# Two kinds of copies on ScalarE placed elsewhere in the attention loop of a gated cross-attention block with a mixture of experts

## What is computed

```python
x = x + tanh(g_xattn[0]) * xattn(layernorm(x), ctx, Wq, Wk, Wv, Wo, q_norm_w, k_norm_w, pos_ctx, pos_x)
x = x + tanh(g_ffn[0])  * ffn(layernorm(x), w_router, w_gate, w_up, w_down, ws_gate, ws_up, ws_down)

# xattn: 16 query heads of 128 in 4 groups, one key head and one value head for each group
q = rope(rms_norm((x_n @ Wq.T) per head)); k = rope(rms_norm((kv_in @ Wk.T) per head)); v = kv_in @ Wv.T
probs = softmax(q @ k.T * SCALE);  out = (probs @ v) @ Wo.T       # kv_in = [ctx, x_n], 128 keys
```

## Time and profile before

| | |
|---|---|
| median of three runs | 1299.71 us |
| the profiled execution | 1300.9 us, of which the span from the first to the last instruction is 1299.1 us |
| granted clock of PE over the span | 0.988 |
| PE busy | 1217.7 us (94%) |
| DVE busy | 1051.7 us (81%) |
| ACT busy | 869.2 us (67%) |
| POOL busy | 962.5 us (74%) |
| share of PE in the chain that ended last | 88% |

### The profile page before, as it was taken

How to read it: one execution, slowest core, us unless ns; L and a number is a source line. 1 busy time by engine, 2 the same in 40 slices (tenths; PEclk the granted TensorE clock), 3 DMA queues, 4 the chain that set the end, 5 groups by cost and what they waited for, 6 DMA issues and landing times.

```text
span 1299.1 us, 31482 instructions
## 1 busy us (share of the span) xinstructions
PE 1217.7 (94%) x8825; PEld 1152.5 (89%) x8826; DVE 1051.7 (81%) x3015; ACT 869.2 (67%) x3745; POOL 962.5 (74%) x1143
## 2 busy tenths in 40 slices
PE   0399999999999999999999999999999889999998
PEld 0389999999999999999999999999999789999898
DVE  8878888888888888888888888888888477777444
ACT  4577777777677777777777777777777436666322
POOL 7577888888887888888888888878887315555554
PEclk9799999999999999999999999999999899999999
DMA  5512222233233322222323333322235826554574
GB/s 190 166 34 71 90 86 89 85 92 105 89 100 108 91 85 85 85 89 88 95 91 90 110 103 97 110 83 71 71 108 172 274 67 187 165 159 150 171 236 142
DMA packets 127093, 148.78 MB, mean 115 GB/s; under 512 B 13760, under 2 KB 107328, under 8 KB 126016
## 3 DMA queue, kind: packets, MB, share of 16 engines
q1 hardware_dynamic: 112192, 126.10, 32.2%
q0 software_dynamic: 6528, 17.90, 3.6%
q10 hardware_dynamic: 8320, 4.19, 1.1%
HBM read 67.26 MB, written 80.89 MB: 114 GB/s over the span
## 4 chain that ended last, share of the span: by engine, by line
PE 88%; DVE 5%; ACT 3%; issue 2%; DMA 1%; POOL 1%; SPq 0%; ACTq 0%; DVEq 0%; POOLq 0%
PE b_q L1583 13%; PE b_kv L1597 13%; PE b_o L1648 13%; PE b_sc L1622 10%; PE b_aT L1637 8%; PE b_pT L1630 5%; PE b_qT L1611 4%; PE b_q L1826 3%; PE b_kv L1826 3%; PE b_aT L1758 3%; PE b_q L1740 2%; PE b_kT L1607 2%; PE b_sc L1740 2%; DVE sincos L413 1%; PE b_aT L1843 1%
## 5 line engine op out<-in xcount | busy, mean ns | idle before, releaser
L1597 PE MATMUL b_kv<-w_group,kv_in_hi 128*128 128x256 f32 x1024 | 212.9, 306 | 9.8 <-DVE k_sin L1184 9.8
L1583 PE MATMUL b_q<-w_group,kv_in_hi 128*128 128x512 f32 x512 | 173.9, 421 | 32.0 <-DVE kv_in_lo L1170 29.3
L722 POOL TENSOR_TENSOR qk_r<-qk_me,minus_half 128x6 f32<-128x6 f32 x128 | 176.4, 1378 | 10.0
L1597 PEld LDWEIGHTS b_kv<-w_group,kv_in_hi 128*128 128x128 f32 x1024 | 168.2, 191 | 17.4 <-DVE k_sin L1184 10.5
L939 ACT ACTIVATE probs<-b_sc,neg_max 128x128 f32<-128x128 f32 x512 | 180.1, 371 | 1.7 <-DVE neg_max L1208 1.7
L726 POOL TENSOR_TENSOR q_rot<-q_rot,q_sin 128x512 f32<-128x512 f32 x128 | 163.5, 1277 | 3.4
L933 ACT ACTIVATE pT<-b_pT 128x512 f32<-128x512 f32 x128 | 76.6, 598 | 133.0 <-PE b_pT L1630 131.1
L1648 PE MATMUL b_o<-wo_hi,aT_hi 128*128 128x256 f32 x512 | 153.9, 301 | 0.2 <-issue 0.2
L1622 PE MATMUL b_sc<-kT,qT 128*128 128x128 f32 x1024 | 139.6, 279 | 12.7 <-issue 6.3
L1597 PE MATMUL b_kv<-w_group,kv_in_lo 128*128 128x256 f32 x512 | 144.8, 283 | 0.0
L1622 PEld LDWEIGHTS b_sc<-kT,qT 128*128 128x128 f32 x1024 | 124.4, 191 | 21.8 <-issue 21.5
(11 more groups left out here) (252 smaller groups left out, 4057.5 us busy)
## 6 DMA issues: line engine op xcount, KB each, us to landing
xs_scratch<-zeros SPq DMA_DIRECT2D x34, 1032.0 KB, 6.2
s_in<-xs_scratch SPq DMA_DIRECT2D x72, 129.0 KB
yT_scratch<-yT SPq DMA_DIRECT2D x32, 256.0 KB
yS<-yT_scratch SPq DMA_DIRECT2D x32, 256.0 KB
routed<-ys_scratch SPq DMA_DIRECT2D x32, 256.0 KB, 3.5
w_hi_all<-w_scratch SPq DMA_DIRECT2D x3, 1536.0 KB, 9.8
x_in<-in_x SPq DMA_DIRECT2D x32, 128.0 KB, 2.2
ctx_raw<-in_ctxT SPq DMA_DIRECT2D x32, 128.0 KB, 2.3
```

Source lines behind the costliest of these rows:

```text
L722: nc.gpsimd.tensor_tensor(qk_r[g % 2][:], qk_me[:], minus_half[:, 0:REP + NB], ALU.pow).then_inc(r_ready, 1)
L1583: last = nc.tensor.matmul(b_q[:], kv_in[p][a][:, c, 1:3, :], wq_of(b, gg)[:, c, :], start=(c == 0 and (a, b) == PASSES[0]), stop=(c == DC ...
L1597: last = nc.tensor.matmul(b_kv[:, s * 2 * HD:(s + 1) * 2 * HD], kv_in[p][a][:, c, 2 * s:2 * s + 2, :], wkv_of(b, c)[:, g % KVH, :], start= ...
```

## The change

`normalize_first` of unit `n` no longer stands at the end of unit `n` on ACT, ahead of the squares of the queries, but in unit `n+1`, behind `values_out`. `piece_hi` no longer ends `g` = 1, but stands behind it in `g` = 2. Only the very last unit keeps its normalisation at its end. Nothing else is changed, no instruction is added or taken away, and no other engine's order changes.

```diff
@@ scalar block, pair @@
                     queries_out(n, g)
                     if not (end and g == 3):
                         values_out(n + 1, g + 1)
+                    if not (first and u == 0):
+                        normalize_first(n - 1, g - 1)
+                    if g == 2 and part is not None:
+                        piece_hi(t, i, p, part)
                     if g == 0 and not end:
                         context_hi(t + 1, i + p, 1 - p)
...
                     if not (first and u == 0):
                         attended_hi(n - 1, g - 1)
-                    normalize_first(n, g)
                     if first and u == 0:
                         split_hi(pieces[9:10])
                     if not (end and g >= 2):
                         query_squares(n + 2, g)
                     if g == 3 and not (first and p == 0):
                         lead_tanh(t - 1)
-                    if g == 1 and part is not None:
-                        piece_hi(t, i, p, part)
+                    if end and g == 3:
+                        normalize_first(n, g)
```

## The result

The changed kernel takes 1284.74 us (median of 4 runs, 1283.72 to 1285.53), the kernel before 1299.7 us in the same rounds: a ratio of 0.9886, with a 95% interval of 0.9875 to 0.9898. It is 15 us faster; 1285.2 was forecast. The profiled execution took 1284.96 us (span 1283.2), 15.9 less than that of before. The sum came out right, but two of its terms were far off, in opposite directions, and a third didn't come.

A forecast was written before the change was run, and what follows sets the result against it. PE (94% busy) was taken to bound the kernel, waiting for the scores in tiles with a piece. Savings of 10.1 (440 columns), 4.6 (608) and 0.4 us (start), less 0.6, gave -14.5: 1285.2 us, range 1278.5 to 1293.

The forecast's parts named there:

- g = 2: Unit g = 2 of tiles with a piece: `qT` starts earlier, saving 0.31 us a tile (440 columns) or 0.46 (608).
- g = 3: Unit g = 3 of tiles with a piece: POOL's `sin_w` ends earlier, saving 0.32 us a tile (440 columns) or 0.12 (608).
- I take tile 26 as the pattern of every tile: g = 3: POOL's timing as in tile 26, without a piece, leaving the scores 0.14 us late (440 columns) or 0.34 (608).
- Rival A: g = 0: DVE's product waits for POOL's `cos_w`, 0.55 us a tile; chance 0.13 in part of the tiles, 0.07 in all.
- +0.6 for one tile or so: Allowance in the sum for about one tile in which DVE newly loses the port to POOL: 0.6 us.
- The start: First pair, where a copy of a projection weight piece stands behind ACT's first normalisation: -0.4 us, between 0 and -0.9.
- The tiles without a piece show no wait: Attention tiles without a piece: PE doesn't wait for the engines, so moving the normalisation gains nothing there.
- Rival C: g = 3: DVE's subtraction is done during POOL's scatter, ahead of `sin_w`, so g = 3 loses nothing; 1278.2 us, chance 0.10.
- B: Only g = 2 gains and g = 3 keeps its 0.51 us a tile; 1290.7 us, chance 0.12.
- D: Nothing moves PE, as something unseen takes the scores' place in both units; 1299.7 us, chance 0.05.

The follow-up runs named there:

- experiment 1: The kernel before with the piece's copy alone moved to g = 2, the normalisation staying at the end of its unit; ratio 0.9892, 1287.97 us.
- experiment 9: The kernel before with the piece moved to g = 2 and, of the normalisations, only that of g = 1; ratio 0.9844, 1278.69 us.
- experiment 2: The kernel before with the normalisation alone moved, the piece's copy still ending g = 1; ratio 0.9936, 1293.8 us.
- experiment 7: The kernel before with only the normalisation of g = 3 moved, behind the values' copy of g = 0; ratio 1.0024, 1303.13 us.
- experiment 8: The changed kernel with the normalisation of g = 3 put back at the end of its unit; ratio 0.9844, 1279.14 us.
- experiment 6: The kernel before with one more small ACT instruction ahead of the exponentials in g = 0, to delay DVE's product; ratio 1.0076, 1309.17 us.
- experiment 12: The kernel before with POOL's `sin_w` in g = 1 and four small DVE multiplications behind `keys_out` in g = 2; single execution, 1299.55 us.
- experiment 4: The kernel before with two short DVE memsets of an unused tile between the reciprocal and the product in g = 0; ratio 1.0005.
- experiment 3: The changed kernel with POOL's two small `layer_rstd` instructions ahead of `cos_table` in g = 0, so `cos_w` starts later; ratio 0.9944, 1294.16 us.
- experiment 5: The kernel before with one 128x128 DVE memset of an unused tile behind the product's wait in g = 0; ratio 1.0005.
- experiment 11: The kernel before with POOL's `sin_w` moved to g = 1, between `key_sum` and the scatter; ratio 0.9982.

## Why the prediction was right in its sum, and where its steps were not

- **g = 2: right.** -8.4 us against -8.6. The 0.31 and 0.46 us were ACT's, the place behind the values' copy is free, and nothing behind it came late.
- **g = 3: right mechanism, size half.** The step that failed is "I take tile 26 as the pattern of every tile". That pattern holds where the normalisation still stands ahead of the squares: 0.25 and 0.11 us in experiment 1, against 0.32 and 0.12 forecast. With the normalisation of g = 1 away as well POOL is another 0.2 us earlier, also in tiles without a piece, so that the scatter starts before DVE's product instead of behind it and takes 1.07 us instead of 1.33. The two together bring `sin_w`'s end from 1.30 to 0.80 us, below what the scores need. So g = 3 gave all of its 0.51 us, in every tile with a piece but tile 2. Experiments 1 and 9 show that this one normalisation does it once the piece is moved (experiment 2: moved alone, it leaves 7.75 us with 440 columns). That the shorter scatter is a part of how is read from the traces, tile 2 among them.
- **Rival A: right mechanism, under-priced.** "+0.6 for one tile or so" was +6.8 us in 11 tiles. The prediction had this very case, 8 to 15 tiles at 0.55 us, and gave it 0.13. The argument against it, that POOL's sum waits for DVE's `q_sin` and not for ACT, was read in one tile (27), where it is true: there `cos_w` still starts 0.08 us behind the product. In tiles 4 and 30 and in most other odd tiles the sum had waited 0.01 to 0.07 us for POOL's own `pow` (L722); with earlier squares it starts sooner. In the 11 tiles struck two things use up the margin, which was 0.01 to 0.11 us. The sum, and with it `cos_w`, starts 0.02 to 0.08 us sooner after the unit's first transpose. And in nine of them (all but 9 and 15) the scores, and DVE's product behind them, start 0.04 us later after that transpose, 2.07 us instead of 2.03. Tile 19 shows that both count: there `cos_w` came 0.07 us sooner, as in tile 13 with the same 0.11 us of margin, but the product no later, and the tile was spared with 0.04 us. The second is in no term of the sum, and no run isolates it. Experiments 7 and 8 lay the long products on the normalisation of g = 3, 6 on the order of the two starts.
- **The start: failed.** Of the -0.4 us nothing came: ACT's copy of the weights came sooner, but DVE's subtraction behind it then began while POOL was in its `cos_w` (67.44 + 1.32), and took 0.71 us longer than before. That it waited for `cos_w` is read from the trace; no run isolates it.
- **"The tiles without a piece show no wait": not in tile 1.** Its g = 3 fell from 7.72 to 7.46 us; from tile 26 on, where it was read, it holds.
- **Rival C's ground: misread.** The subtraction had begun 0.43 us ahead of the scatter's end without getting done, and I held that against the inference of the Trainium skill ("SBUF — State Buffer", section "Who interferes with whom") that generating descriptors doesn't stop such an instruction. Experiment 12 agrees with the page in this direction: 0.78 us in nearly the same place. What held it up was `sin_w`, queued behind the scatter. The forecast that the subtraction would still wait for `sin_w` was right all the same.
- **B and D** fell with g = 3. A loss six us larger and a gain six us larger than forecast made the sum look exact; that they cancel is luck.

## What to carry to other kernels

A margin between two engines' starts must be read in every repetition of the loop, not in one: here 17 of 29 tiles had 0.01 to 0.11 us, and where it struck the change took 0.02 to 0.12 of it. When a change bundles the same move at several places, cost each place by itself; one of five moves here lost 6 us of what two others gained, and leaving it out gave 1279 us instead of 1285. An instruction that blocks another can't be put "later" at will: it needs a gap as long as itself, and behind the gap stands the next instruction that it can block.

## What the runs showed of the hardware

- **Queued order, not recorded start.** `sin_w` wins over a subtraction recorded 0.39 us before it when it stands ready behind a scatter, and the product wins over a `cos_w` recorded 0.07 us before it when it stands behind a memset. With nothing of DVE's ahead of the product in line, 0.02 us decide, and a tie went to POOL (experiments 6 and 7); with a memset ahead of it, a tie went to DVE (experiment 4). That an instruction's claim is made when it is issued, while the one ahead of it still runs, fits all of these; the moment itself wasn't measured, and for the memset a claim of its own isn't excluded. The Trainium skill (the section cited above) has the order of issue decide, too.
- **The scatter waits too.** It takes 1.07 us when it starts 0.08 us ahead of DVE's product, 1.33 when it starts 0.16 us behind (the product there at 865.59) and 1.45 when 0.06 behind (tile 2): in both of these it ends 0.93 to 0.95 us after the product. The product takes 0.56 us in all three, so DVE isn't held by it. In this direction the product does hold up the scatter, as the traces have it, while the Trainium skill ("SBUF — State Buffer", section "Who interferes with whom") infers that such an instruction doesn't stall the generation of descriptors; no run tests this alone.
- **PE's clock at the start.** In the profiled executions of experiments 1, 3, 5, 8 and 11 the granted clock of PE was 0.78 to 0.80 between 68.6 and 76.5 us, and unit 1 took 10.0 to 10.3 us; in those of before, of the changed kernel and of experiment 9 it was 1.00 and 7.8. Each has one fall back to the lower level (0.50, 1.2 GHz) in the first two units, at different places. Before, the clock is 1.00 (2.4 GHz) from 62 to 64 us and 0.50 from 64 to 67, in unit 0, after PE had idled 2.2 us for `qT`. In experiment 1 it is 1.00 from 62 to 72 us, through the same idle time (2.0 us), and 0.50 from 73 to 75, in unit 1, after PE had idled 2.1 us for `kT`. So unit 0 takes 7.93 us there instead of 8.78 and unit 1 10.33 instead of 7.83: 1.6 us in all (61.7 against 60.1 for the first eight units). It comes and goes between kernels with the same order there: the changed kernel and experiment 8 differ in nothing that stands before the end of unit 3. Why one execution falls in unit 0 and another in unit 1 stays open.
